# Two six-layer transformer stacks: six query transfers per layer begun by ScalarE, dummy matmuls at other places

## The reference

```
NL, D, H, DFF = (6, 128, 16, 512)       # 6 layers, 16 heads of 8
for i in range(NL):
    xn = _adaln(x, noise_emb, n1_w[i], n1_b[i])             # norm "0"
    q, k, v = split(xn @ qkv_w[i].T);  q = _rope(q); k = _rope(k)
    x = x + _attn(q, k, v, src_mask) @ so_w[i].T            # self attention, 512 keys
    xn = _adaln(x, noise_emb, n2_w[i], n2_b[i])             # norm "1"
    q = _rope(xn @ cq_w[i].T); k = _rope(context @ ck_w[i].T); v = context @ cv_w[i].T
    x = x + _attn(q, k, v, ctx_mask) @ co_w[i].T            # cross attention, 154 keys
    xn = _adaln(x, noise_emb, n3_w[i], n3_b[i])             # norm "2"
    x = x + (gelu(xn @ f1_w[i].T + f1_b[i]) @ f2_w[i].T + f2_b[i])
```

## Time and profile before

| | us |
|---|---|
| median of 3 runs | 3594.2 |
| lowest and highest of them | 3593.28, 3600.89 |
| the profiled execution's own time | 3588.33 |
| its span, first to last instruction | 3586.5 |
| PE busy | 2955.5 (82%) |
| DVE busy | 2087.1 (58%) |
| ACT busy | 1910.6 (53%) |
| POOL busy | 808.6 (23%) |
| granted TensorE clock, mean | 0.93 |

### The profile page before, as it was taken

How to read it: one execution, slowest core, us unless ns; L and a number is a source line. 1 busy time by engine, 2 the same in 40 slices (tenths; PEclk the granted TensorE clock), 3 DMA queues, 4 the chain that set the end, 5 groups by cost and what they waited for, 6 DMA issues and landing times.

```text
span 3586.5 us, 50572 instructions
## 1 busy us (share of the span) xinstructions
PE 2955.5 (82%) x15567; PEld 1033.0 (29%) x15567; DVE 2087.1 (58%) x3631; ACT 1910.6 (53%) x2693; POOL 808.6 (23%) x1327
## 2 busy tenths in 40 slices
PE   7898999868888787888888747888788787888866
PEld 2463333222222222222222212222222222222225
DVE  4326777457475664846558367557375664746524
ACT  5433333337466574765647434647466474665632
POOL 0003455512222222221212102222212222222211
PEclk9999999779999998998999977999999998999977
DMA  1100000001110101111011001011110101101030
GB/s 42 53 15 10 1 1 1 11 26 36 32 37 26 49 20 36 42 30 39 26 31 39 21 13 41 24 37 34 33 36 27 44 25 32 44 24 47 24 117 7
DMA packets 125570, 110.73 MB, mean 31 GB/s; under 512 B 49982, under 2 KB 116076, under 8 KB 125292
## 3 DMA queue, kind: packets, MB, share of 16 engines
q1 hardware_dynamic: 114924, 97.80, 9.3%
q10 hardware_dynamic: 10368, 9.44, 0.9%
HBM read 41.96 MB, written 0.52 MB: 12 GB/s over the span
## 4 chain that ended last, share of the span: by engine, by line
PE 61%; DVE 17%; issue 7%; ACT 6%; POOL 5%; SPq 2%; DMA 1%; DVEq 0%; ACTq 0%; POOLq 0%
PE ps L517 11%; DVE arena L794 8%; PE ps L462 6%; PE ps L491 4%; PE ps L642 4%; PE ps L584 3%; PE ps L627 3%; ACT arena L667 3%; PE ps L546 2%; PE ps L1486 2%; PE ps L534 2%; PE ps L570 2%; PE ps L525 2%; PE ps L562 2%; PE ps L1474 2%
## 5 line engine op out<-in xcount | busy, mean ns | idle before, releaser
L667 ACT ACTIVATE arena<-ps 128x1024 f32<-128x1024 f32 x960 | 936.8, 1024 | 342.2 <-PE ps L491 338.7
L794 DVE TENSOR_REDUCE arena<-ps 128x1 f32<-128x512 f32 x1536 | 966.5, 685 | 214.5 <-PE ps L462 189.6
L517 PE MATMUL ps<-arena 128*32 128x512 f32 x3840 | 513.7, 609 | 20.5 <-ACT arena L667 18.0
L462 PE MATMUL ps<-arena 49*128 49x512 bf16 x1536 | 316.1, 408 | 253.6 <-DVE arena L794 202.9
L491 PE MATMUL ps<-arena 52*128 52x512 bf16 x1920 | 346.3, 387 | 27.9 <-ACT arena L667 24.7
L796 DVE TENSOR_REDUCE arena<-ps 128x3 f32<-128x462 f32 (+1 forms) x576 | 303.9, 580 | 90.7 <-PE ps L469 87.0
L876 POOL TENSOR_TENSOR arena<-arena,zeros 128x16 bf16<-128x16 f32 x192 | 42.6, 222 | 1051.4 <-DVE arena L794 622.9
L462 PEld LDWEIGHTS ps<-arena 49*128 49x128 bf16 x1536 | 75.1, 94 | 594.8 <-DVE arena L794 490.4
L886 POOL TENSOR_TENSOR arena<-arena 128x512 f32<-128x512 f32 x96 | 122.2, 1273 | 453.4 <-ACT arena L699 453.4
L892 POOL TENSOR_TENSOR arena<-arena 128x512 bf16<-128x512 f32 (+1 forms) x84 | 92.6, 1102 | 548.1 <-ACT arena L726 548.1
L805 DVE TENSOR_TENSOR h<-ps,h 128x512 f32<-128x512 f32 x48 | 33.2, 692 | 293.8 <-PE ps L546 293.8
(11 more groups left out here) (383 smaller groups left out, 4336.2 us busy)
## 6 DMA issues: line engine op xcount, KB each, us to landing
arena<-arena SPq DMA_DIRECT2D x720, 64.0 KB
arena<-we_dram SPq DMA_DIRECT2D x24, 578.5 KB, 7.5
arena<-arena ACTq DMA_DIRECT2D x144, 64.0 KB
w<-weights_dram SPq DMA_DIRECT2D x26, 320.0 KB, 3.1
w<-weights_dram SPq DMA_DIRECT2D x13, 512.0 KB, 3.8
arena<-arena SPq DMA_DIRECT2D x384, 6.0 KB
arena<-arena SPq DMA_DIRECT2D x288, 19.2 KB
w<-weights_dram SPq DMA_DIRECT2D x39, 128.0 KB, 2.1
```

The lines of the kernel that those rows point to most:

```text
L462: pe.matmul(s_bank(slot + r), qst[b][rows, idx, P * qt:P * (qt + 1)], kst[b][rows, idx, :], start=True, stop=True).then_inc(s_full, 1 + (z ...
L517: mm = pe.matmul(bank(7)[32 * j:32 * j + 32, :], v, prob[:, slot, j, :], start=(g % 2 == 0 and kt == 0), stop=(a == 0 and g % 2 == 1 and k ...
L667: act.activation(prob[:, chunk_no(b, a, g, kt) % NPROB, 2 * p:2 * p + 2, :], e_bank(slot).rearrange("p (j n) -> p j n", j=2), ACT.Exp, sca ...
L794: op = ve.tensor_reduce(nmax[:, g % 2, r, n:n + 1], s_bank(slot + r), AX.X, ALU.max, negate=True)
```

## The change

Three edits, all in the code that both stacks share.

1. `("st", 0, 0, 0)`, the six transfers of part 0 of batch 0's self queries, joins `ACT_STACKS`. ACT begins them at place -17, and SP no longer does.
2. `FILL` gives two fillers to `("score", 1, 1, 0, 0)`, the first cross score of batch 1, and one to `("center", 0, 2)`, the third norm of batch 0; `("out", 1, 1)` has two, not three.
3. `score`, `center_h` and `var` get the code that runs fillers. In `score` they stand behind the wait for free banks and ahead of the wait for the stacking.

```diff
-        ACT_STACKS = (("st", 0, 1, 0), ("st", 1, 2, 0))
-        FILL = {("out", 0, 1): 3, ("out", 1, 1): 3, ("f1", 0, 0): 1}
+        ACT_STACKS = (("st", 0, 0, 0), ("st", 0, 1, 0), ("st", 1, 2, 0))
+        FILL = {("out", 0, 1): 3, ("out", 1, 1): 2, ("f1", 0, 0): 1, ("score", 1, 1, 0, 0): 2, ("center", 0, 2): 1}
...
             def score(it):
                 _, b, a, g, n = it
+                if it in FILL:
+                    pe.wait_ge(s_free, z.room("s", it, 2))
+                    fill(it, s_bank(z.use("s", it)[0]))
                 if g == 0 and n == 0:
                     pe.wait_ge(stacked_q[b], z.ahead(f"q{b}", it))
...
             def center_h(it):
                 _, b, k = it
                 slot, at = z.use("e", it)
+                if it in FILL:
+                    pe.wait_ge(e_free, z.room("e", it, 1))
+                    fill(it, e_bank(slot)[:, 0:S])
...
             def var(it):
                 _, b, k = it
                 slot, at = z.use("e", it)
+                if it in FILL:
+                    pe.wait_ge(e_free, z.room("e", it, 1))
+                    fill(it, e_bank(slot)[:, 0:S])
```

## The result

| | before | after |
|---|---|---|
| median, us | 3593.8 | 3634.1 |
| lowest and highest of 4 runs each | 3593.28, 3600.89 | 3631.82, 3637.59 |
| the profiled execution's own time | 3588.33 | 3634.04 |
| its span | 3586.5 | 3632.2 |
| granted TensorE clock, mean | 0.93 | 0.919 |

The ratio is 1.0116, with a 95% interval of 1.0102 to 1.0129: the change costs 40 us, or 1.2%. The forecast was 3631 in a range of 3604 to 3652.

A forecast was written before the change was run, and what follows sets the result against it. The prediction took ACT's chain of exponentials and transfers to L546 to bound each layer boundary. Hold +34, clock +9, lead-ins -3 and fillers -3 made +37 us on 3594.2, so 3631, range 3604 to 3652.

The forecast's parts named there:

- What bounds the boundary: Ten layer boundaries: a chain through ACT's exponentials to L546 ends last, the stacking at none of them.
- Rival 3: Boundaries: stacking is the bound after all, hidden in "issue" waits; up to 2 us each back, 3611; within the 0.76.
- The hold: Ten boundaries: six more transfers ahead of tail's exponential delay ACT's chain by 3.4 us each, +34 us.
- Rival 2: Boundaries: ACT's issue does not hold the chain, so they cost nothing; -10 us, 3584; faster 0.07, same 0.06.
- The clock: PE's longer gap at ten boundaries brings half clock to L517 and L525: 0 to +1.9 us each, +9 in all.
- I take the middle: Clock term at the boundaries: 0.9 us each taken, +9 us in all, with 0 and +19 as ends.
- The lead-ins: Two stack lead-ins: ACT and SP share the issuing, last issue 2.0 us earlier; 1.7 gained each, -3 us.
- The fillers: First cross score, center and out: full clock around f1 in three layers; -3 us, between -6 and +4.
- L546 waited 0.20 us for POOL with three fillers in front; it was not held by them, so two give nothing: out(1,1) at the end of a layer: dropping its third filler gains no time except possibly clock.
- rival 1: Boundaries: delay stays, clock does nothing or all, 3618 to 3651; with faster issue on ACT 3606; within the 0.76.

The follow-up runs named there:

- e10: Kernel before with only out(1,1) cut from three fillers to two, no new fillers: 3588.0 us, ratio 0.9990.
- e1: Kernel before with ACT beginning the six transfers of the queries' part 0, fillers as before: 3639.2 us, ratio 1.0129.
- e5: Changed kernel, but SP begins the keys' part 0, so ACT has only the queries' six, ahead of tail: 3635.1 us, ratio 1.0131.
- e4: Changed kernel, but of the six transfers of the queries' part 0 ACT begins two and SP four: 3609.7 us, ratio 1.0039.
- e3: Changed kernel plus four fillers per layer ahead of batch 1's last exp matmul, in PE's gap: 3629.4 us, ratio 1.0103.
- e11: Changed kernel plus four fillers ahead of the last exp matmul, except in each stack's last layer: 3619.5 us, ratio 1.0067.
- e9: Kernel before with the changed fillers, plus four more behind the first score at the loop's turns: 3590.8 us, ratio 0.9991.
- e2: Kernel before with the changed fillers only, stacking as before; run twice: 3580.3 us (ratio 0.9959) and 3583.1 us (0.9967).
- e6b: Changed kernel, but ACT begins the queries' part 0 only in the two lead-ins, SP at the boundaries: 3584.5 us, ratio 0.9983.

## Why the prediction was right, and where it was not

**What bounds the boundary** was read rightly: the stacking ended last at none of them. After the change L465's waits have this row,

```profile
  DMA arena<-arena: 25.9, 3
```

and the two lead-ins are nearly all of it, as in the earlier trace rows. So the sooner stacking gave nothing that this row shows. Rival 3 had it hidden behind "issue", and that wait did get shorter in the first stack; but it did so in e10 too, which has the old stacking, and not in e1, which has the new one (3.6 to 3.7 us there for 3.6 to 3.9). So rival 3 falls.

**The hold** was the main term, 10 x 3.4. It measured 3.53 at `tail` and 3.25 at the last `pv`, 1.5 us less over the ten. e5 shows that it belongs to the place ahead of `tail`, and e4 that it falls with the number of transfers (0.56 us for two, 0.6 worked out beforehand). Rival 2 had the page of the Trainium skill named in the prediction beside it (DMA: Bandwidth & Descriptors, "Issuing engines are not separate DMA queues"). The trace differs from its word "small" where the engine has compute behind the issue: six issues took 4.28 us, and L685 stood 3.47 us for them. Beside the transfer itself one issue was not small either: 0.7 us, where 1.7 to 3.1 us passed in the lead-ins from the end of the last issue to the score.

**The clock** was the term that was mis-sized: 0.9 us a boundary, in a range of 0 to 1.9, and the runs show 1.4 (e3, and e11 from `pv` to `evac`) to 1.5 (the table). The working up to the range holds. At the boundary shown, L520 and L528 together took 5.34 us (2599.38 to 2604.72), where the rows before have 2.78, which is 2.6 more as the prediction said. At full clock L695 would have begun 0.17 us behind ACT's transfers, as in e3, at 2602.86; it began 1.93 us later, so 0.6 to 0.7 of the 2.6 was hidden and the upper end of the range was reached. The step that failed is "I take the middle": the clock fell at all ten boundaries, and `evac` came at 11.36 to 12.42 us behind the zero, where it came at 10.25 to 10.52 at eight of e3's. 5 to 6 us were missing.

**The lead-ins** were given 1.7 us each and gave 0.9. The last issue ended 2.3 us sooner behind the first one (I had said 2.0), but from there to the score it took 3.14 us instead of 1.73, which took 1.4 back. That two issuers at once make the transfers land later, as the prediction feared, fits this, but no run takes it apart. The bound of 0 to 2.0 held it.

**The fillers** were given -3 in all, -6 to +4. Beside edit 1 the difference of after to e1 is -5; by themselves they gave -12. Their mechanism came true where they stand, full clock at `f1` in all layers, but no trace shows the 2 us in each of three layers as time. The step that failed is "L546 waited 0.20 us for POOL with three fillers in front; it was not held by them, so two give nothing". At the loop's turns two instead of three give 1.5 us where the long wait for "issue" was, 4.6 us in all. The 2.05 us before the score stood in the earlier trace rows, and I took it as fixed; the other stack's turns had 3.6 to 3.9.

So the sum of +37 against +40 measured is partly luck: 6 us of clock and 1 of lead-ins were missing, and 1.5 of hold and 2 of fillers were too many. One sum within rival 1 is off: with a shift of 2.4 us in place of 3.4 its lower end is 3618 - 10 = 3608, not 3606; nothing else hangs on it but the lower edge of the forecast.

## What to carry to other kernels

A transfer is begun by an engine in its own order, and each issue held ACT for 0.7 us; before moving transfers to another engine, read what compute stands behind them there and who waits for it, and put a group only where the engine has that much idle time. A gap that opened on PE cost twice here, once as the wait (3.3 us) and again as matmuls at half clock behind it (1.4 to 1.5), and the second part was bought back with fillers placed in the gap. Fillers can also only move the half clock to another place: 51 us less of it gave no time in e9. So cost them as a range, time the parts apart, and do not read the gain of a few us out of one trace.

## What was not expected of the hardware

- A gap of 1.9 to 2.3 us on PE, up from 1.57, went with half clock on `pv` at all ten boundaries of e4 (3.4 us each), where the kernel before had none. In e11 it was the same at two boundaries, where the gap was 2.0 and 2.1, and at none of the eight where it was 1.1 to 1.3.
- The wait for "issue" at a turn of the loop has two sizes, 1.9 to 2.7 and 3.5 to 3.9 us, the same at all three turns of a stack except once (e11), and one dummy matmul more or fewer at the end of the loop's turn changes how often it is long (9 of 18 turns with three, 1 of 60 with two). That it has to do with how PE gets its instructions at the jump is a guess that no run tests.
- The same items after the same work had the clock at half for 3.4 us in one kernel and 10.2 us in another that ran 1.6 us later. This remains open, and with it the fillers' gain, -12 us in e2 and -6 in e6b: nothing in the order of the work tells the two apart there, and no run here varies the one and holds the other.
